# A 3x3 convolution kernel: the last columns of the first store cut as 112 rows of 1792 bytes instead of 126 rows of 1536

## The reference

```python
def _gn(v, G=16, eps=1e-5):
    g = v.reshape(B_, G, C_ // G, H_, W_)
    m = jnp.mean(g, axis=(2, 3, 4), keepdims=True)
    s = jnp.var(g, axis=(2, 3, 4), keepdims=True)
    return ((g - m) / jnp.sqrt(s + eps)).reshape(v.shape)
...
px = jnp.pad(x, ((0, 0), (0, 0), (0, fft_H - H), (0, fft_W - W)))
fx = jnp.fft.fft2(px, norm='ortho')
wf = jnp.fft.fft2(pw, norm='ortho')
fout = jnp.einsum('bihw,oihw->bohw', fx, wf)
sp = jnp.fft.ifft2(fout, norm='ortho').real
out = sp[:, :, sh:sh + out_h, sw:sw + out_w]
return out + bias[None, :, None, None]
...
x = x + _L0_conv_ref(_gn(x), L0_conv_weight, L0_conv_bias, 1, 1)
```

## Time and profile before

| | |
|---|---|
| time, median of 3 runs | 82.91 us |
| the profiled execution's own time | 83.1 us |
| its span, first to last instruction | 81.9 us |
| TensorE matmul busy | 66.6 us, 81% |
| VectorE, ScalarE, GpSimd busy | 50.2, 47.9, 31.6 us |
| queue of SP's DMAs (q1) | 2164 packets, 33.36 MB, 96.1% of 16 engines' span |
| queue of GpSimd's DMAs (q0) | 96 packets, 0.19 MB, 0.7% |

### The profile page before, as it was taken

The page is one execution under the profiler, slowest core; times in us unless marked ns, Lnnn a source line. Parts: engine busy times, 40 slices in busy tenths (PEclk is TensorE's granted clock), DMA queues, the critical chain, the costliest instruction groups (busy, mean ns, idle before and its releaser), DMA issues.

```text
span 81.9 us, 685 instructions
## 1 busy us (share of the span) xinstructions
PE 66.6 (81%) x222; PEld 41.1 (50%) x222; DVE 50.2 (61%) x43; ACT 47.9 (59%) x53; POOL 31.6 (39%) x43
## 2 busy tenths in 40 slices
PE   0009965999999999999999999999999999993000
PEld 0005424566666666666666656666565656660000
DVE  0009936961899499679949985995899324006000
ACT  3307967991799299569948965994798350000000
POOL 6994000004069910106996930490095039100000
PEclk9999997589999999999999999999999999999965
DMA  0999999999989988999897998979969999989996
GB/s 21 318 424 460 440 408 448 432 416 448 536 352 448 496 352 384 455 442 455 344 541 336 488 444 352 481 320 512 496 272 472 424 384 472 424 384 480 385 408 264
DMA packets 2309, 33.62 MB, mean 411 GB/s; under 512 B 313, under 2 KB 347, under 8 KB 645
## 3 DMA queue, kind: packets, MB, share of 16 engines
q1 hardware_dynamic: 2164, 33.36, 96.1%
q0 software_dynamic: 96, 0.19, 0.7%
q10 hardware_dynamic: 48, 0.06, 0.4%
HBM read 16.84 MB, written 16.78 MB: 411 GB/s over the span
## 4 chain that ended last, share of the span: by engine, by line
PE 75%; DMA 14%; DVE 2%; SPq 1%; issue 0%; POOL 0%; POOLq 0%
PE ps L417 73%; DMA x<-x_dram 14%; DVE x L433 2%; PE ps_m L323 1%; SPq L184 1%; PE ps_w L269 1%; POOL pair L217 0%; POOL eps L188 0%; POOLq L587 0%
## 5 line engine op out<-in xcount | busy, mean ns | idle before, releaser
L417 PE MATMUL ps<-g,w_sb 128*128 128x363 f32 (+1 forms) x192 | 60.5, 471 | 0.0
L417 PEld LDWEIGHTS ps<-g,w_sb 128*128 128x128 f32 x192 | 35.9, 194 | 19.8 <-ACT origin L297 1.4
L287 DVE TENSOR_REDUCE sums<-x 128x1 f32<-128x4096 f32 x7 | 30.9, 4410 | 0.6 <-DMA x<-x_dram 0.6
L399 POOL TENSOR_SCALAR x<-x,bias_sb 128x1984 f32<-128x1984 f32 (+3 forms) x12 | 23.2, 1942 | 18.1 <-ACT origin L297 13.7
L308 ACT ACTIVATE unused<-x,origin 128x4096 f32<-128x4096 f32 (+1 forms) x9 | 30.0, 3334 | 0.3
L433 DVE SCALAR_TENSOR_TENSOR x<-ps,bias_sb,x 128x1089 f32<-128x1089 f32 (+2 forms) x9 | 10.9, 1220 | 7.7 <-PE ps L417 7.7
L378 ACT ACTIVATE g<-x,rstd 128x1089 f32<-128x1089 f32 (+2 forms) x8 | 9.4, 1188 | 3.4 <-DVE rstd L352 3.4
L287 DVE TENSOR_REDUCE first_sums<-x 128x1 f32<-128x2048 f32 x2 | 4.6, 2286 | 6.2 <-DMA x<-x_dram 6.2
L262 POOL COPY sums<-x 128x1 f32<-128x1 f32 x6 | 1.0, 184 | 18.7 <-DMA x<-x_dram 18.7
L269 PE MATMUL ps_w<-x,avg 128*128 128x1 f32 x4 | 1.1, 341 | 7.1 <-POOL w_sb L486 6.1
L340 DVE TENSOR_SCALAR var<-ps_m,square 128x1 f32<-128x1 f32 x8 | 1.7, 218 | 8.0 <-ACT square L335 8.0
(11 more groups left out here) (21 smaller groups left out, 13.0 us busy)
## 6 DMA issues: line engine op xcount, KB each, us to landing
x<-x_dram SPq DMA_DIRECT2D x3, 2048.0 KB, 15.4
out_dram<-x SPq DMA_DIRECT2D x3, 2048.0 KB
x<-x_dram SPq DMA_DIRECT2D x1, 4096.0 KB, 29.0
out_dram<-x SPq DMA_DIRECT2D x1, 4096.0 KB
out_dram<-x SPq DMA_DIRECT2D x1, 3904.0 KB
x<-x_dram SPq DMA_DIRECT2D x1, 3328.0 KB, 36.4
x<-x_dram SPq DMA_DIRECT2D x2, 1024.0 KB, 6.0
out_dram<-x SPq DMA_DIRECT2D x1, 1056.0 KB
```

What stands on the lines that cost most here:

```text
L287: lambda e: e.tensor_reduce(to_sum(img, k)[:, 0:1], piece, mybir.AxisListType.X, ALU.add),
L399: put("pool", lambda e: e.tensor_scalar(part, part, 1.0, bias_sb, op0=ALU.mult, op1=ALU.add), *free, mark=mark)
L417: lambda e, k=k, dc=dc, rows=rows, top=top: e.matmul(ps[:, 0:rows, 0 : N - dc], w_sb[:, k * P : (k + 1) * P], g[:, top : top + rows, dc:N] ...
```

## The change

REST goes from 6 to 7 and MOST from 126 to 112. The large SP store now carries 7744 numbers of each of 128 rows instead of 7808. GpSimd's store carries 112 rows of 448 numbers (1792 bytes), seen as 14 x 8 rows, instead of 126 rows of 384 numbers (1536 bytes), seen as 42 x 3; it is issued with `single_packet=True`. SP's small store carries the last 16 rows of 448 numbers instead of the last 2 rows of 384. The host's reordering follows.

```diff
-    REST = 6
-    MOST = 126
+    REST = 7
+    MOST = 112
...
     def store(to, of, *needs, by="sp"):
-        return put(by, lambda e: e.dma_start(to, of), *needs, adds="moved" if by == "pool" else "stored")
+        if by == "pool":
+            return put(by, lambda e: e.dma_start(to, of, single_packet=True), *needs, adds="moved")
+        return put(by, lambda e: e.dma_start(to, of), *needs, adds="stored")
...
-                    spread = flat(out[0])[0:MOST, most:].rearrange("(b a) n -> a b n", b=3)
+                    spread = flat(out[0])[0:MOST, most:].rearrange("(b a) n -> a b n", b=8)
                     moved = store(spread, flat(pairs[0])[0:MOST, most:], *biased[1], turned, by="pool")
...
-    last = out[0, :126, 1, -6:]
-    last[:] = last.reshape(3, 42, *last.shape[1:]).transpose(1, 0, 2, 3).reshape(last.shape)
+    last = out[0, :112, 1, -7:]
+    last[:] = last.reshape(8, 14, *last.shape[1:]).transpose(1, 0, 2, 3).reshape(last.shape)
```

## The result

The changed kernel takes 83.28 us (median of 6 runs, 83.18 to 83.40), the kernel before 82.93 us beside it (6 runs, 82.90 to 83.05). The ratio is 1.0040, with a 95% interval of 1.0029 to 1.0050: slower by 0.35 us, where no change was forecast and 83.05 was the upper end.

A forecast was written before the change was run, and what follows sets the result against it. The 16 DMA engines were taken as the bound throughout. Per engine, -0.076 (large store) - 0.04 (GpSimd's store) + 0.08 (small store) = -0.04 us, so 82.91 becomes 82.87 us, "the same"; range 82.65 to 83.05.

The forecast's parts named there:

- Step (a): SP's large store: 8 rows per engine of 30976 instead of 31232 bytes, saving 0.076 us on all 16 engines.
- Step (c): SP's small store: one more 1792-byte row and its completion on every engine, 0.066 to 0.150 us, taken as 0.08.
- Step (b): GpSimd's store: 14336 bytes in one packet per engine instead of 13824 in three, from -0.10 to +0.02 us, taken as -0.04.
- loss end: GpSimd's store at its worst: excess stays in proportion to the bytes, 0.66 us against 0.635, a loss of 0.02.
- the interference of 0.12 us: GpSimd's store before the change: three packets took 0.635 us together against 0.512 at full rate; interference or packet cost.
- Rival C: GpSimd's store: `single_packet` changes nothing in the packets, or cuts each row into its own; 82.93 us, chance 0.07.
- Rival B: SP's 16-row small store collides with itself on neighbouring partitions: 0.26 us instead of 0.08, time 83.05 to 83.11, chance 0.10.
- one burst with little excess: GpSimd's third burst before the change: packets of three 1536-byte rows took 0.184 us against 0.171 at full rate.
- point of decision: SP's small store: "slower" begins at 83.08 us, from 0.29 us per small row, or 0.23 with GpSimd's store at its loss end.
- Rival D: At the kernel's end, another engine becomes the slowest by chance, moving the time 0.1 us either way; chance 0.08.

## Why the prediction was wrong

**What bounds the kernel: right.** The 16 DMA engines; TensorE's end moved by 1.1 us without effect, and the last store stood in the queue.

**Step (a), the large store: right.** -0.076 us forecast, -0.090 measured. The closeness is partly luck: profiles with the same large store differ by 0.1 us in its sum (9.50 before, 9.40 in the kernel before without small store). The least row fell from 1.156 to 1.147, 0.072 for eight.

**Step (c), the small store: failed, by its size.** "I take 0.08, near the lower end" of 0.066 to 0.150; it measured 0.193 us per row, beyond the upper end too (0.163 in the profile without the flag). The rows that bounded it, small packets of the weights and large rows at full rate, say nothing of 16 rows of neighbouring partitions read at once. That where the rows lie bears on the price is shown for whole rows (92.25 against 88.89 us); for the small ones it is argued from that.

**Step (b), GpSimd's store: failed, by its sign.** -0.04 us forecast with a loss end of +0.02; per engine that has a packet it went from 0.647 us (3 x 0.216) to 0.796 (42 x 0.265 / 14), +0.15. Other profiles with the same store give 0.581 and 0.612 before, and 0.728 and 0.792 after, so that the sign is sure and the size is 0.08 to 0.22. I read the interference of 0.12 us as something that the bytes or the packets' number bring. What the runs show instead is that the layout bears on it: 8 rows per engine do worse than 9 or 7 (112 rows against 126 and 98, at two widths), the 9 with more bytes. The sentence that each engine would get "8 rows of 1792 bytes" was right, the one packet of 14336 bytes was not: what Rival C said of the flag is what happened, and its price (82.93) failed with (b) and (c).

**Rival B** came nearest to the mechanism: 16 engines that want neighbouring partitions at one time. It got 0.10 because I set one burst with little excess against it, but those were packets of GpSimd's 9-row layout. Its point of decision, 0.23 us per small row with (b) at its loss end, was not reached (0.193); the loss came with less of it and more of (b).

**Together:** the forecast for an engine with GpSimd's packets was -0.04 us; by the same steps, measured, it is -0.09 + 0.15 + 0.19 = +0.25, and the time moved by 0.35. With the profile without the flag the same sum is -0.08 + 0.08 + 0.16 = +0.16, at the same 83.28 us. The rest is the matter of Rival D, which I took to move the time either way: in both profiles of the changed kernel one engine ends 0.20 to 0.26 us behind the next, while before the last two are 0.01 apart. Why it is one engine, and whether the collisions fall on it, stays open.

The Trainium skill's page "SBUF — State Buffer", section "Door 1: The DMA port swizzle", which puts partitions 112 to 127 on 4 of 16 ports, fits the direction of these comparisons: neighbouring rows worse than rows 8 apart (92.25 against 88.89 us). By its formula the first rows of 14 blocks of 8 partitions lie on 8 ports, with two blocks on six of them, those of blocks of 9 on 14 different ones, and those of blocks of 7 on 12. It doesn't give the sizes (8.1 us where four in turn would be 4.9). That the port is what collides isn't shown by any row; what is shown is that the choice of source partitions alone changes the time.

Of the kernels that compute everything none was faster than the kernel before.

## What to carry to other kernels

When the DMA engines are the bound, price a transfer per engine, and ask which partitions all engines read at the same moment. In this kernel SP's full 128-row stores ran at the least time of their packets (32768 bytes: 1.216 us on the mean, 1.213 at least), and a 16-row piece of neighbouring partitions, a 112-row store of SP, or a block of 8 rows per engine on GpSimd's queue did not. A packet's duration over that of a free one of its size (here 0.193 us against 0.074) shows that engines are held up; a busy share doesn't (1.00 at 274 GB/s, 0.94 at 405). Look at the last completions one by one as well, since the time is that of the last engine.

## What I had not expected

- The same 16 rows of 32768 bytes, one on each engine, took up to 8.1 us each when read from partitions 112 to 127, and the kernel was 9.3 us longer than before.
- A store of 112 rows (7 per engine) from SP took 1.404 us per row of 30976 bytes, one of 128 rows 1.176.
- GpSimd's queue cut its rows into packets of three (4608 or 5376 bytes) with a rest of two, with `single_packet` and without (112 rows); rows of 7168 bytes went one by one.
- Without any split, with the least work per engine, the time ranged from 82.81 to 83.61 us, while the kernel before stayed within 82.75 to 83.24 beside it. In the one execution with a profile one engine ended 0.48 us behind the next.
